# A fused four-layer graph network on one core: the first layer's second norm folded into the MLP weights, its third norm adding the input

## The reference

```python
h  = layernorm(L_norm @ x @ Wc + bc) * g1 + be1         # first norm; L_norm = 2 L / lam_max - I
x1 = relu(h) + x
o  = attention(x1; Wq, Wk, Wv, 4 heads, masked) @ Wo + bo
x2 = layernorm(x1 + o) * g2 + be2                       # second norm
m  = gelu(x2 @ W1 + b1) @ W2 + b2                       # 256 -> 512 -> 256
y  = layernorm(x2 + m) * g3 + be3                       # third norm
x  = layernorm(x + y)                                   # fourth norm, without scale or bias
```

## Time and profile before

| | us |
|---|---|
| median of three runs | 2298.62 (2295.13 to 2299.04) |
| span of the profiled execution | 2298.5 |
| first layer, from PE's first product to its last | 43.00 to 674.60 |
| PE busy in 43 to 675 | 592.17 |
| DVE busy in 43 to 675 | 504.90 |
| ACT, POOL busy in 43 to 675 | 292.83, 257.13 |

### The profile page before, as it was taken

One profiled execution on the slowest core, in us unless ns is written; L12 is line 12 of the kernel. 1 busy time (PEld: TensorE's weight loads), 2 busy tenths in 40 slices (PEclk: granted clock), 3 DMA queues, 4 the chain that ended last, 5 costly groups with the idle time before them and its releaser, 6 DMA issues. The chain is left out here.

```text
span 2298.5 us, 44203 instructions
## 1 busy us (share of the span) xinstructions
PE 2138.9 (93%) x17360; PEld 1878.8 (82%) x17360; DVE 1384.4 (60%) x2703; ACT 1153.9 (50%) x2183; POOL 440.6 (19%) x876
## 2 busy tenths in 40 slices
PE   4999999999969989999999999999999797979998
PEld 3888888888869978888888889988888786858886
DVE  4788788878866644443344434354443677956776
ACT  1444454355433357644444534443533565648886
POOL 3344344434430000000000000000000221014554
PEclk9999999999999999999999999999999899989999
DMA  3110111011013201000000000000000331001221
GB/s 99 34 56 19 41 50 55 9 46 55 28 40 109 63 30 37 1 19 1 1 1 19 19 1 1 1 1 1 1 1 1 114 119 60 1 28 60 79 76 51
DMA packets 76401, 81.86 MB, mean 36 GB/s; under 512 B 6544, under 2 KB 74000, under 8 KB 75408
## 3 DMA queue, kind: packets, MB, share of 16 engines
q1 hardware_dynamic: 76304, 80.51, 11.1%
HBM read 55.33 MB, written 25.17 MB: 35 GB/s over the span
## 5 line engine op out<-in xcount | busy, mean ns | idle before, releaser
L323 PE MATMUL ps<-R 128*128 128x256 f32 (+3 forms) x8136 | 1494.5, 344 | 38.5 <-DVE R L1545 12.9
L323 PEld LDWEIGHTS ps<-R 128*128 128x128 f32 x8136 | 1313.5, 191 | 202.1 <-DVE R L802 15.7
L1226 ACT ACTIVATE late_half<-ps,lstm_bias 128x512 f32<-128x512 f32 (+2 forms) x460 | 283.4, 669 | 382.1 <-PE ps L323 382.0
L365 POOL TENSOR_TENSOR ln_veps<-ln_mv,eps_tile 128x2 f32<-128x2 f32 x128 | 28.6, 223 | 1313.9 <-DVE ln_mv L348 1313.9
L864 PE MATMUL ps<-H 128*128 128x256 f32 x1024 | 238.3, 382 | 3.1 <-ACT H L785 1.7
L864 PEld LDWEIGHTS ps<-H 128*128 128x128 f32 x1024 | 188.9, 191 | 26.5 <-ACT H L785 1.9
L1261 DVE TENSOR_TENSOR late_half<-late_half 128x1024 f32<-128x1024 f32 (+2 forms) x32 | 37.6, 1176 | 186.4 <-ACT late_half L1226 186.4
L1223 ACT ACTIVATE late_half<-late_half 128x1024 f32<-128x1024 f32 (+2 forms) x66 | 68.1, 1032 | 124.4 <-DVE late_half L1266 78.4
L1263 DVE TENSOR_TENSOR late_half<-late_half 128x1024 f32<-128x1024 f32 (+2 forms) x32 | 37.6, 1176 | 132.6 <-ACT late_half L1226 132.6
L391 DVE SCALAR_TENSOR_TENSOR H<-H,ln_rstd 128x256 f32<-128x256 f32 x192 | 106.5, 595 | 6.8 <-POOL ln_rstd L358 3.3
L1270 DVE TENSOR_TENSOR H<-late_half 128x1024 f32<-128x1024 f32 (+2 forms) x34 | 45.9, 1349 | 89.9 <-ACT late_half L1226 89.9
(11 more groups left out here) (211 smaller groups left out, 2668.7 us busy)
## 6 DMA issues: line engine op xcount, KB each, us to landing
H<-in_x SPq DMA_DIRECT2D x64, 256.0 KB, 4.1
residual<-H SPq DMA_DIRECT2D x32, 256.0 KB, 2.2
H<-residual SPq DMA_DIRECT2D x32, 256.0 KB, 4.0
arena<-residual SPq DMA_DIRECT2D x32, 256.0 KB, 2.8
residual<-arena SPq DMA_DIRECT2D x32, 256.0 KB, 2.2
H_state<-residual SPq DMA_DIRECT2D x32, 256.0 KB, 2.7
out<-H_state SPq DMA_DIRECT2D x32, 256.0 KB, 2.2
arena<-in_wih SPq DMA_DIRECT2D x4, 1024.0 KB, 4.8
```

Of the source, the lines that this page charges most:

```text
L323: mm = pe.matmul(out, lhsT(a), rhs(b), start=start and n == 0, stop=stop and n == len(PASSES) - 1)
L1226: ins = act.activation(into[q][:, m, 0:x.cols], gate_ps(q, m, x.cols), ACT.Tanh if q == TANH_G else ACT.Sigmoid, bias=lstm_bias[:, x.p - 1 ...
```

## The change

It does five things.

1. The second norm's result is kept as plain normalized rows z (mean taken off, times rstd), by a new function `ln_normalize`: one `tensor_scalar` per tile (L388 of the changed kernel) in the place of L386 and L391. Scale and bias go elsewhere: `W1 := g2 * W1` by rows (two ACT instructions in the setup, L552), and `b1 := b1 + be2 @ W1` (eight one-column products on PE, L656, put between the fourth and the fifth of the six runs of squarings, and one DVE addition).
2. The residual is now made from z on POOL by two instructions in slot 13, `z * g2` and then `+ (b2 + be2)` (L773, L775), where one stood (L742). The row `b2 + be2` is made once in the setup.
3. The addition of x on POOL behind the third norm (L746, slot 16) goes. In its place POOL adds be3 to x beforehand, in a new slot 12 (L778), and the third norm's second instruction (L401) adds that sum where it added be3.
4. The statistics of slot 17 on DVE now stand at the end of slot 16; POOL's slot 17 moves from tick 119 to 112. SP's slot 4 waits for y_made in the place of yx_ready.
5. In the setup W1 and the new columns (`ln2c`, 128 x 4 numbers) are loaded ahead of the other weights.

```diff
+    def ln_normalize(dve, y, s, rstd, count):
+        dve.wait_ge(rstd, count)
+        for n in range(TILES):
+            ins = dve.tensor_scalar(y[:, n, :], y[:, n, :], ln_mv[:, s, n, 0:1], ln_rstd[:, s, n:n + 1],
+                                    ALU.subtract, ALU.mult)
+        return ins
...
+            act.wait_ge(w1_loaded, 2 * 16)
+            act.wait_ge(b1_made, 1)
+            for k in range(KD):
+                act.activation(W1[:, k, :], W1[:, k, :], ACT.Copy, scale=ln2_col[:, 0, k:k + 1]).then_inc(w1_scaled, 1)
...
+            squarings(0, SQUARINGS // RUN - 2)
+            pe.wait_ge(w1_loaded, 2 * 16)
+            for m in range(HID0 // P):
+                for k in range(KD):
+                    mm = pe.matmul(ps0(6)[:, m:m + 1], W1[:, k, m * P:(m + 1) * P], ln2_col[:, 1, k:k + 1],
+                                   start=(k == 0), stop=(k == KD - 1))
+            mm.then_inc(b1_made, 1)
+            squarings(SQUARINGS // RUN - 2, SQUARINGS // RUN)
...
-        dve={1: 26, 2: 31, 3: 35, 6: 51, 8: 60, 11: 77, 12: 80, 13: 85, 15: 100, 16: 104, 17: 111},
-        pool={1: 29, 3: 45, 11: 78, 13: 80, 15: 104, 16: 108, 17: 119},
+        dve={1: 26, 2: 31, 3: 35, 6: 51, 8: 60, 11: 77, 12: 80, 13: 85, 15: 100, 16: 104},
+        pool={1: 29, 3: 45, 11: 78, 12: 86, 13: 80, 15: 104, 17: 112},
...
                 if slot == 13:
                     pool.wait_ge(x_ready[s], 2 * turn + 2)
                     pool.wait_ge(y_stored[s], 16 * turn + 16)
-                    pool.tensor_tensor(x2b_t[s], hb_t[s], over_tiles(b2), ALU.add).then_inc(biased_ready[s], 1)
-                if slot == 16:
-                    pool.wait_ge(y_made[s], turn + 1)
+                    c = steps.enter(s, slot, turn)
+                    c.step(pool.tensor_tensor(x2b_t[s], hb_t[s], over_tiles(g2), ALU.mult))
+                    c.settle()
+                    pool.tensor_tensor(x2b_t[s], x2b_t[s], over_tiles(b2), ALU.add).then_inc(biased_ready[s], 1)
+                if slot == 12:
                     pool.wait_ge(xr0_loaded[s], 16 * turn + 16)
-                    pool.tensor_tensor(y_t[s], y_t[s], xr0_t[s], ALU.add).then_inc(yx_ready[s], 1)
+                    pool.tensor_tensor(xr0_t[s], xr0_t[s], over_tiles(be3), ALU.add).then_inc(x_be3[s], 1)
...
                 if slot == 12:
-                    ln_affine(dve, c, hb_t[s], s, g2, be2, var_ready[s], rstd_ready[s], 2 * turn + 2)\
-                        .then_inc(x_ready[s], 1)
+                    ln_normalize(dve, hb_t[s], s, rstd_ready[s], 2 * turn + 2).then_inc(x_ready[s], 1)
...
                 if slot == 16:
-                    ln_affine(dve, c, y_t[s], STREAMS + s, g3, be3, var2_ready[s], rstd2_ready[s],
+                    dve.wait_ge(x_be3[s], turn + 1)
+                    ln_affine(dve, c, y_t[s], STREAMS + s, g3, xr0_t[s], var2_ready[s], rstd2_ready[s],
                               2 * turn + 1, 2 * turn + 3).then_inc(y_made[s], 1)
-                if slot == 17:
-                    dve.wait_ge(yx_ready[s], turn + 2)
+                    c.settle()
+                    dve.wait_ge(y_made[s], turn + 2)
                     ln_statistics(dve, c, y_t[s], STREAMS + s, var2_ready[s])
```

More of the change, by code:

```diff
@@ L165, in build_program @@
     b1_col = sb("b1_col", [P, HID0 // P])
+    ln2_col = sb("ln2_col", [P, 2, KD])
     MB = HID2 // P
@@ L390, in ln_affine @@
         for n in range(TILES):
-            ins = dve.scalar_tensor_tensor(out=y[:, n, :], in0=y[:, n, :], scalar=ln_rstd[:, s, n:n + 1], in1=be,
+            ins = dve.scalar_tensor_tensor(out=y[:, n, :], in0=y[:, n, :], scalar=ln_rstd[:, s, n:n + 1], in1=be[:, n, :],
                                            op0=ALU.mult, op1=ALU.add)
@@ L463, in _ @@
             sp.dma_start(scal[:, 1:2], rows("gamma")).then_inc(small_loaded, 16)
-            for dst, name in ((Wc, "Wc"), (Wq, "Wq"), (Wk, "Wk"), (Wv, "Wv"), (Wo, "Wo"), (W1, "W1"), (W2, "W2")):
+            for dst, name in ((W1, "W1"), (ln2_col[:], "ln2c")):
+                sp.dma_start(dst, t[name]).then_inc(w1_loaded, 16)
+            for dst, name in ((Wc, "Wc"), (Wq, "Wq"), (Wk, "Wk"), (Wv, "Wv"), (Wo, "Wo"), (W2, "W2")):
                 sp.dma_start(dst, t[name]).then_inc(w0_loaded, 16)
@@ L619, in _, with squarings @@
               .then_inc(small_mm, 1)
[L620 to L628, removed]
+            def squarings(first, last):
+                with pe.Fori(first, last) as i:
+                    for r in range(RUN):
+                        pe.wait_ge(p_ready, RUN * i + r + 1)
+                        alone(pe, waits_passed)
+                        pe.matmul(ps0(3)[0:NODES, 0:NODES], P64[0:NODES], P64[0:NODES], start=True, stop=True)\
+                          .then_inc(squared, 1)
+                    pe.wait_ge(q_ready, i + 1)
+                    pe.matmul(ps0(4)[:, 0:1], ones[0:NODES, :], col[0:NODES, 12:13],
+                              start=True, stop=True).then_inc(tr_ready, 1)
+            squarings(0, SQUARINGS // RUN - 2)
[6 more added lines that the diff above has]
+            squarings(SQUARINGS // RUN - 2, SQUARINGS // RUN)
             pe.wait_ge(spread_asked, 1)
@@ L678, in build_program @@
      var_ready, rstd_ready, x_ready, biased_ready, qkv_done, qkv_ready, sc_done, sc_ready, exp_ready, at_ready,
-     atT_ready, up_done, gelu_ready, var2_ready, rstd2_ready, y_made, yx_ready, y_ready, y_stored) = (sems(n) for n in
+     atT_ready, up_done, gelu_ready, var2_ready, rstd2_ready, y_made, x_be3, y_ready, y_stored) = (sems(n) for n in
                   ("xr0_loaded", "mixed", "mixed_ready", "product_done", "turned",
@@ L720, in _ @@
         def _(pool):
-            steps = Steps(pool, "l0_pool", {1: 1, 11: 1})
+            steps = Steps(pool, "l0_pool", {1: 1, 11: 1, 13: 1})
             tail = Steps(pool, "l0_pool_tail", {15: 1, 17: LN_SHIFT})
-            ahead(pool, yx_ready)
             def stage(s, slot, turn):
@@ L793, in _ @@
         def _(dve):
-            steps = Steps(dve, "l0_dve", {1: 1 + LN_STATS, 2: LN_AFFINE, 8: 2, 11: 1 + LN_STATS,
-                                          12: LN_AFFINE - 1})
-            tail = Steps(dve, "l0_dve_tail", {15: 1 + LN_STATS, 16: LN_AFFINE - 1, 17: LN_STATS})
+            steps = Steps(dve, "l0_dve", {1: 1 + LN_STATS, 2: LN_AFFINE, 8: 2, 11: 1 + LN_STATS})
+            tail = Steps(dve, "l0_dve_tail", {15: 1 + LN_STATS, 16: LN_AFFINE - 1 + LN_STATS})
             ahead(dve, var2_ready, by=2)
+            ahead(dve, y_made)
             def split_lo(s, count, half):
@@ L1817 @@
     lay["b1"] = columns(a["L0_gnn_b1"])
+    lay["ln2c"] = np.stack([columns(a["L0_gnn_g2"]), columns(a["L0_gnn_be2"])], 1)
     lay["Wg0"], lay["Wg1"] = split_rows(a["L1_gnn_Wg0"]), split_rows(a["L1_gnn_Wg1"])
```

14 lines of the change are left out of this document (10 added, 4 removed).

## The result

The changed kernel takes 2321.51 us (median of 4 runs, 2320.26 to 2322.84) against 2298.66 before: a ratio of 1.0099, 95% interval 1.0084 to 1.0113. The forecast was 2300.6, range 2291.5 to 2308, so the time lies outside it.

The account below looks back on a forecast made before the run. PE bounds the kernel, and only its waits, mostly on late DVE results, can be won. From 2298.5: rounds - 0.3, setup + 3.8, layer end - 1.5 give 2300.5, median 2300.6 us; range 2291.5 to 2308.

Parts of the forecast that it names:

- The rounds: First layer's seven rounds, five taken as cold: + 0.6, less 0.9 for D's extra occurrence, together - 0.3 us.
- D: PE's wait of 0.92 us for slot 12 of s3; forecast to go.
- C: PE's wait of 0.78 us for slot 2 of s0; forecast to go.
- E: New PE wait of 1.4 us early in the round: s2's statistics now stand ahead of slot 2 of s3.
- A: PE's wait for the low part of s2; forecast 2.2 us in place of 1.73.
- The clock behind A: 24 PE products behind A take 3.13 us warm or 4.50 cold; five of seven rounds taken as cold.
- my case: Main forecast for the whole kernel: + 2.0 us, from - 2.9 to + 6 by clock and setup bounds; chance 0.48.
- The slower rival: POOL's new slot 12 ahead of s3's rstd lengthens E and A: 2309.5 us, or 2305 at half price; chance 0.30.
- The faster rival: DVE's relief decides: E vanishes, A stays 1.73, C and D go; 2289 us, 2294 with E halved; chance 0.22.
- The setup: One-column products in the squaring chain cost 4.0 us, 3.3 net; setup in all + 3.8, bounds 0 and + 5.
- The end: First layer's end: DVE's 1.68 us wait for POOL's sum goes, but for some 0.15: - 1.5 us.
- The new instruction: DVE's slot 12: a pair of tensor_scalar takes 0.6 us, between 0.35 and 0.88, with no stall counted.

Follow-up runs that it names:

- e1: Kernel before plus one unused 8-word tensor where the change puts its column tensor, no instruction changed; 2314.6 us, ratio 1.006.
- e7: Kernel before with 8 unused words ahead of the LSTM's two upper tensors, moving operands 32 bytes up; 2315.7 us, ratio 1.006.
- e5: Changed kernel with the new columns in unused bytes behind the bias columns, so no other tensor moves; 2307.1 us, ratio 1.0019.
- e6: e5 with the last statistics taken out of slot 16 into their own slot 17 at tick 111; 2290.8 us, ratio 0.9953.
- e2: Changed kernel with 24 unused words behind the new column tensor, no instruction changed; 2320.8 us, ratio 1.008.
- e4: e2 with the last statistics taken out of slot 16 into their own slot 17 at tick 111; 2303.2 us.

## Why the prediction was wrong, step by step

**The step that failed** is the sum: "2298.5 - 0.3 + 3.8 - 1.5 = 2300.5" has a term for the setup, the rounds and the end of the first layer, and none for the other three layers. I took it as given that code which the diff doesn't touch keeps its time. In its place the runs show 11.7 us in the LSTM (899.93 less 888.20) from the distance of two addresses, shown by e1 and e7 alone and given back in e5. With the 6.8 us of the first layer and nothing else the time would have been 2305.3, inside the range. Of the 14.6 us behind the first layer 4.2 lie between its end and the first of the LSTM's listed issues (906.82 less 692.97 is 213.85, before 209.62). e5, without the shift, has 1.4 of them, and e1, with the shift alone, 1.3; so has e7, where nothing moves before the LSTM. What makes the remaining 1.5 stays open.

**The rounds** were forecast at - 0.3 and measured at + 4.9 (from PE's first product to its last group: 45.74 to 678.53, before 43.00 to 670.88). The pieces:
- D is gone, C is gone, and E is new with 1.22 in the first round and 1.41 to 1.51 in the six others (forecast 1.4). These three were right, and C's cause too: the pair that POOL stalled before takes 0.87 in the change (at 394.45), and in e6, where it is stalled again, C is back. So was E's working: from the L876 that PE releases to the end of L851 DVE takes 12.40 us (433.23 to 445.63) for 12.29 forecast, and e6, which takes the statistics away, has no wait there. The stall of 0.55 that was counted into E is absent in e6 too, so the two are not told apart.
- A was forecast at 2.2 and is 2.87. The sentence "it gains the statistics of s0 and has lost those of s2; what remains is E's lateness and one more dependent start" netted two things that do not net. PE's place is set anew by its wait at E; from there to A the statistics of s0 come on top, 1.06 us in the rows at 380.79. From E's transposes to A PE takes 15.95 us (366.62 to 382.57) in place of 15.14 (360.83 to 375.97), and it does its work between them without the wait of 0.18 that it had there. A grew by 1.14; in e6 it is back at 1.72.
- The clock behind A: five cold rounds of seven were assumed at the old price of 4.50. Six of seven were below full clock, and two stood at the 1.2 GHz level for the whole group with 5.49 us. The longer wait made the products behind it dearer, as the counts over all traces show (1 of 28 groups at full clock, 52 of 112 behind the shorter wait); the forecast held that price fixed.

- The range of my case, "- 2.9 to + 6", does not come out of its own terms: all warm with the setup at 0 gives - 6.8, all cold with the setup at 5 gives + 5.2. The forecast does not hang on it.

**The slower rival** gave 2309.5 by POOL's new slot 12. One sign that it named did come: POOL's rstd for s3 is late. DVE's timeline, with POOL's two L778 from 422.32 to 425.03 beside the first row:

```profile
422.72 2.60 DVE L396 SCALAR_TENSOR_TENSOR H<-H,ln_mv 128x256 f32<-128x256 f32 x2
426.25 0.88 DVE L401 SCALAR_TENSOR_TENSOR H<-H,ln_rstd 128x256 f32<-128x256 f32 x2 [0.94 <-POOL ln_rstd L360]
...
433.23 0.69 DVE L876 TENSOR_TENSOR H<-ps,H 128x512 f32<-128x512 f32 x1 [1.34 <-PE ps L896]
```

The pair is stalled by 1.7 us, and the next one waits 0.94 for rstd. But by 433.23 DVE waits for PE again, for 1.34 us, so PE loses nothing by it, as the prediction had placed it ("nothing lost"). e6 has the same two rows (2.60 and 0.94) and gains all the same. L778 also stalls one pair behind 433.23, by 0.55 us (1.42 in place of 0.87, at 437.37), as assumed for E.

**The faster rival** (2289 by relief of DVE) had E gone, A at 1.73, and C and D gone, 12 us in the rounds. e6 has the first, second and fourth, and C stays with 1.06: its rounds take 617.7 us (45.59 to 663.30), 10.2 less than before. Its condition was slack of DVE, and that was there once the statistics were not moved. That e6 stands at 2290.8, so near to 2289, is in part luck: the kernel before stood 3.6 us higher beside it than in the comparison that was forecast.

**The setup** was forecast at + 3.8 and is + 2.74 (45.74 less 43.00). The block took 3.58 us for 4.0 forecast, 0.22 a load. The row of the same stretch was near it. By the Trainium skill's figure for a load (TensorE: Matmul & The Clock Gate, section "LDWEIGHTS") the block was an estimated 1.7 us, half of what it took; the measurement decides.

**The end** was forecast at - 1.5. POOL's wait is gone, but in the change the joined statistics of one group stand ahead of the last group's sum, and only 0.9 is gained (20.26 from the last group to the next layer, before 21.13). e6, with the statistics apart, gains 1.6 (19.5).

**The new instruction.** All 64 of it, in the changed kernel:

```profile
L388 DVE TENSOR_SCALAR H<-H,ln_mv,ln_rstd x64: 405/407/415, 91.4 to 669.3; 128x256 f32<-128x256 f32 x64
```

In the timeline a pair takes 0.73 to 0.74 us, where the pairs of L386 and L391 took 0.88 each; forecast 0.6 between 0.35 and 0.88. None was stalled (415 ns at most). In the round from 405 to 432 us no wide POOL instruction runs beside any of them, as forecast, so whether one would stall them was not tested. DVE's busy time fell by 24 us (504.9 to 481.3 over the layer), forecast 30 to 40; POOL's rose by 44 (257.1 to 300.7), forecast 40.

## What to carry to other kernels

A new tensor moves all that is allocated behind it. When a stretch that nobody edited changes its rate with the granted clock at 1.00 and no waits, compare the tensors' addresses first; one unused tensor in the old kernel shows it in a run. Put small new tensors where nothing moves, or at the end.

Statistics or any other work that nobody waits for soon does not belong in a slot that stands ahead of an operand that PE waits for; joining two slots cost more (16.3 us between e5 and e6, 17.6 between e2 and e4) than the whole change could gain (11.5 in e6).

When DVE's relief is the aim, measure the fold by itself: here the rounds' gain was all the fold's, and it outweighed the 2.7 us of setup.

## What the runs showed of the hardware

In this LSTM, PE's rate in back-to-back products depends on the distance between the SBUF address of the weights and that of the moving operand. Ten shifts from 0 to 256 bytes gave 225 ns (0 and 256) to some 233 ns (160) a product of 512 columns; at 256, three of the four stretches agreed with before to 0.03 us. Products of 462 columns went the other way at a shift of 32 (374 to 368 ns), and their stretch took 66.2 us at 16, 32, 96, 128, 160 and 192 bytes and 67.6 to 67.7 at 0, 64, 224 and 256. The Trainium skill (SBUF — State Buffer, section "Who interferes with whom") gives TensorE two independent read ports and says that it never waits on another engine. It says nothing of a distance between them; here the two reads of one engine do not look independent. That they meet in the memory behind the ports is my reading and was not shown: ScalarE and VectorE write into both tensors now and then, and no run took that away. Open too: why e2 and e4, with the same addresses, differ by 2.5 us in the LSTM, and the order of the rates within the period.
